# One layer (Mamba-2 mixer and top-2 LoRA feed-forward) on one core: in the first token block ScalarE makes the skip terms of chunks 2 and 3, and steps are put in another order

## What is computed

```
xn  = layernorm(x)
out = x + attn(xn) + ffn(xn)

attn: proj = xn @ in_proj_w.T            -> gate 4096, conv input 6144, dt 64
      xBC  = silu(conv4(conv input))     -> x (64 heads x 64), B, C (8 groups x 128)
      state_t = state_{t-1} * exp(dt A) + dt x_t B_t ;  y_t = state_t C_t
      y  = y + x * D                     (D: one number a head, the skip term)
      yn = rmsnorm over 512 (y) * norm_weight * silu(gate) ; attn = yn @ out_proj_w.T
ffn:  xn @ W_base.T + b + top-2 of 8 experts of rank 16 (scale 2)
```

## Time and profile before

| | us |
|---|---|
| median of three runs | 3119.39 (3118.51 to 3121.8) |
| the profiled execution, its own time | 3118.07 |
| its span in the trace | 3116.3 |
| TensorE busy | 3098.2 (99%) |
| VectorE busy | 2681.8 (86%) |
| ScalarE busy | 1787.1 (57%) |
| GpSimd busy | 813.7 (26%) |

### The profile page before, as it was taken

How to read it: one execution, slowest core, us unless ns; L and a number is a source line. 1 busy time by engine, 2 the same in 40 slices (tenths; PEclk the granted TensorE clock), 3 DMA queues, 4 the chain that set the end, 5 groups by cost and what they waited for, 6 DMA issues and landing times.

```text
span 3116.3 us, 55148 instructions
## 1 busy us (share of the span) xinstructions
PE 3098.2 (99%) x17392; PEld 2547.4 (82%) x17392; DVE 2681.8 (86%) x4675; ACT 1787.1 (57%) x4782; POOL 813.7 (26%) x833
## 2 busy tenths in 40 slices
PE   8999999999999999999999999999999999999999
PEld 7788888887888888888788888888878888888887
DVE  7998888987598999999759899999975899999984
ACT  5766666664256665566326666655633656666651
POOL 4444443434022222212203122222110211221210
PEclk9999999999999999999999999999999999999999
DMA  8777777776665555565566555555646655556554
GB/s 286 277 263 274 270 271 273 261 264 248 241 228 191 195 201 188 192 203 192 181 224 205 196 193 193 202 190 190 215 164 229 212 190 196 196 195 201 192 190 163
DMA packets 185670, 672.63 MB, mean 216 GB/s; under 512 B 21056, under 2 KB 22208, under 8 KB 185408
## 3 DMA queue, kind: packets, MB, share of 16 engines
q1 hardware_dynamic: 161280, 584.91, 53.8%
q10 hardware_dynamic: 24128, 84.42, 8.3%
HBM read 532.41 MB, written 136.84 MB: 215 GB/s over the span
## 4 chain that ended last, share of the span: by engine, by line
PE 90%; DVE 6%; ACT 2%; issue 1%; DMA 1%; SPq 0%; ACTq 0%; DVEq 0%
PE dense L1157 20%; PE dense L1159 19%; PE dense L1158 19%; PE pX L1157 7%; PE pX L1159 7%; PE pX L1158 7%; PE pY L1271 3%; DVE conv_us L1572 3%; PE pD L1271 1%; PE pCB L1244 1%; PE pS L1158 1%; PE pS L1157 1%; PE pS L1159 1%; PE pU L1157 1%; PE pU L1159 1%
## 5 line engine op out<-in xcount | busy, mean ns | idle before, releaser
L1157 PE MATMUL dense<-xn_hi,w_hl 128*128 128x512 f32 (+2 forms) x2192 | 868.3, 396 | 2.2 <-ACT conv_us L725 1.3
L1159 PE MATMUL dense<-xn_hi,w_hl 128*128 128x512 f32 (+2 forms) x2192 | 853.1, 389 | 0.0
L1158 PE MATMUL dense<-xn_lo,w_hl 128*128 128x512 f32 (+2 forms) x2192 | 851.9, 389 | 0.0
L1572 DVE SCALAR_TENSOR_TENSOR conv_us<-conv_in,const_g,conv_us 128x512 f32<-128x512 f32 x576 | 469.5, 821 | 30.2 <-ACT conv_us L725 18.4
L1157 PEld LDWEIGHTS dense<-xn_hi,w_hl 128*128 128x128 f32 (+1 forms) x2192 | 409.8, 187 | 92.5 <-ACT conv_us L725 4.8
L1159 PEld LDWEIGHTS dense<-xn_hi,w_hl 128*128 128x128 f32 (+1 forms) x2192 | 409.5, 187 | 88.1
L1158 PEld LDWEIGHTS dense<-xn_lo,w_hl 128*128 128x128 f32 (+1 forms) x2192 | 410.0, 187 | 85.8 <-issue 2.6
L1607 DVE STREAM_TRANSPOSE x_tm<-xBC 32x320 f32<-32x320 f32 x832 | 417.8, 502 | 12.8
L520 POOL TENSOR_TENSOR C_lo<-xBC,C_hi 128x128 fp32r<-128x128 f32 x120 | 66.0, 550 | 1207.6 <-ACT S_hi L768 1207.2
L1757 DVE STREAM_TRANSPOSE xBC<-yn 32x256 f32<-32x256 f32 x672 | 292.9, 436 | 77.9 <-ACT yn L845 67.6
L1157 PE MATMUL dense<-z_hi,w_hl 128*128 128x512 f32 x820 | 326.5, 398 | 1.9 <-DVE acc L1780 1.1
(11 more groups left out here) (239 smaller groups left out, 5673.5 us busy)
## 6 DMA issues: line engine op xcount, KB each, us to landing
w_hl<-w_split SPq DMA_DIRECT2D x732, 512.0 KB, 3.5
w_split<-w_hl SPq DMA_DIRECT2D x244, 512.0 KB, 3.8
cum_b<-cum_scratch ACTq DMA_DIRECT2D x128, 512.0 KB, 5.0
w_raw<-w_slots_dram SPq DMA_DIRECT2D x122, 512.0 KB, 5.5
acc<-x_tr_dram ACTq DMA_DIRECT2D x16, 512.0 KB, 6.5
out_tr_dram<-acc ACTq DMA_DIRECT2D x16, 512.0 KB, 4.7
xBC<-x_tok_dram SPq DMA_DIRECT2D x6, 512.0 KB, 5.3
conv_us<-x_tok_dram SPq DMA_DIRECT2D x6, 512.0 KB, 6.1
```

Of the source, the lines that this page charges most:

```text
L1157: nc.tensor.matmul(out, lhs[0], rhs[0], start=start, stop=False)
L1158: nc.tensor.matmul(out, lhs[0], rhs[1], start=False, stop=False)
L1159: return nc.tensor.matmul(out, lhs[1], rhs[0], start=False, stop=stop)
L1572: nc.vector.scalar_tensor_tensor(out=conv_u[r], in0=conv_in[r][:, t:t + TB], scalar=const_g[p][:, 4 * j + t:4 * j + t + 1], in1=conv_u[r], ...
```

## The change

It has four parts.

1. **Skip terms.** In block 0, for chunks 2 and 3 of groups 1 to 7, VectorE's one instruction of 128x512 (L1665) goes, and ScalarE makes the same xD by eight instructions of 128x64, one a head, the head's D as scale (`skip_one`). They stand behind `normalize` and ahead of the next `split`. That is 14 instructions less on VectorE and 112 more on ScalarE.
2. **Silu and evacuation.** In groups 1 to 6 VectorE runs the silu of unit j-1 ahead of the taps of unit j, and ScalarE the evacuation of unit j ahead of the tanh of unit j-1.
3. **Groups 1 and 7.** Group 1: ScalarE normalizes chunk 3 of group 0 before it evacuates gate unit 1, and makes its z_hi before the next split; VectorE makes its z_lo before the next low half, and its rounds of `x_rows` stand one each in the output units 1 to 3. Group 7: the rounds stand in the output units 0 to 2 instead of one ahead of them and two in them.
4. **End.** The last of the four stores is cut in two, one tile each.

The diff:

```diff
@@ -427,7 +427,7 @@
                 block_body(q, False, False)
             block_body(NQ - 1, False, True)
 
-            sp.wait_ge(out_stored, 16 + NQ * 64)
+            sp.wait_ge(out_stored, 16 + NQ * 64 + 16)
 
 
         @block.gpsimd
@@ -688,6 +688,9 @@
             nc.scalar.activation(A_neg[:], A_neg[:], ACT.Exp).then_inc(const_act, 1)
 
             def block_body(q, first_block, last_block):
+                def skip_by_act(g, c):
+                    return first_block and turned(g, c, first_block)
+
                 n_dt = 0
 
                 def dt_step(ins):
@@ -812,6 +815,8 @@
                     wx_high(g, c)
                     if c >= 1:
                         normalize(g, c - 1)
+                    if skip_by_act(g, c):
+                        skip_one(g, c)
                     next_cum(g, c, last)
 
                 def skip(g, c):
@@ -820,6 +825,14 @@
                     act.wait_ge(y_x, carry_n(q, g, c, False) - (1 if g == 1 and c == 0 else 2))
                     for h in range(HPG):
                         ins = nc.scalar.activation(xD_2[c % 2][:, h * P:(h + 1) * P], x_tm[:, c % 2, h * P:(h + 1) * P], ACT.Copy,
+                                                   scale=D_g[:, h:h + 1])
+                    ins.then_inc(xd_done, 1)
+
+                def skip_one(g, c):
+
+                    act.wait_ge(xt_done, xt_n(q, g, c, first_block))
+                    for h in range(HPG):
+                        ins = nc.scalar.activation(xD[:, h * P:(h + 1) * P], x_tm[:, c % 2, h * P:(h + 1) * P], ACT.Copy,
                                                    scale=D_g[:, h:h + 1])
                     ins.then_inc(xd_done, 1)
 
@@ -931,9 +944,9 @@
                             x_conv(j)
                             tanh_conv(g, j - 1)
                         elif not last:
+                            x_conv(j)
                             if j >= 1:
                                 tanh_conv(g, j - 1)
-                            x_conv(j)
 
                     def out_unit(m):
                         if not first:
@@ -943,8 +956,9 @@
                     if behind_first:
                         z_high(0, 2)
                         mean_square(0, 3)
-                        gate_unit(1)
+                        split(g, k_gate(first, 1))
                         normalize(0, 3)
+                        ev_gate(g, first, 1, p)
                     else:
                         if not first:
                             normalize(g - 1, 3)
@@ -952,8 +966,10 @@
                     chunk_1(g, p, 0, last)
                     if first:
                         load_residual(1)
+                    if behind_first:
+                        z_high(0, 3)
                     split(g, k_gate(first, 2))
-                    if not first:
+                    if not first and not behind_first:
                         z_high(g - 1, 3)
                     ev_gate(g, first, 2, p)
                     gate_unit(3)
@@ -1090,6 +1106,12 @@
                         paired_group(g, g % 2, second=g > 1)
                 (group if first_block else paired_group)(7, 1, last=True)
 
+                def store_tile(i):
+
+                    act.wait_ge(evac_dve, tail_n(q, i))
+                    act.dma_start(out_tr[bass.ds(q, 1), :, i:i + 1, :].rearrange("b p o t -> (b p) o t"),
+                                  acc[:, i:i + 1, :]).then_inc(out_stored, 16)
+
                 def store(m):
 
                     act.wait_ge(evac_dve, tail_n(q, 2 * m + 1))
@@ -1109,7 +1131,11 @@
                     ln_high(q + 1, 3)
                 store(1)
                 store(2)
-                store(3)
+                if last_block:
+                    store_tile(OT - 2)
+                    store_tile(OT - 1)
+                else:
+                    store(3)
 
             block_body(0, True, False)
             with act.Fori(1, NQ - 1) as q:
@@ -1661,6 +1690,8 @@
                     nc.vector.tensor_tensor(B_lo[:], pCB[:, 0:N], B_hi[:].bitcast(F32), ALU.subtract).then_inc(bl_done, 1)
 
                 def skip(g, c):
+                    if skip_by_act(g, c):
+                        return
                     dve.wait_ge(sq_done, chunk(q, g, c) + 1)
                     nc.vector.tensor_tensor(heads(xD[:]), heads(x_tok_of(g, c)), D_g[:].unsqueeze(2).broadcast_to([128, HPG, P]),
                                             ALU.mult).then_inc(xd_done, 1)
@@ -1907,10 +1938,12 @@
                             if m == 0:
                                 dve.wait_ge(acc_loaded, (q + 1) * 64)
                             out_adds(g, m, halves=(0,))
-                            if first_block and m < 2:
-                                x_rows(g, 2, p, 2 + m, 3 + m)
+                            row = m + (0 if behind_first else 1 if last else 2)
+                            if 1 <= row < 4:
+                                x_rows(g, 2, p, row, row + 1)
                             out_adds(g, m, halves=(1,))
-                            lo(g, K_OUT + m)
+                            if not (behind_first and m == 0):
+                                lo(g, K_OUT + m)
 
                     def x_low(j):
                         if last:
@@ -1919,9 +1952,9 @@
 
                     def x_conv(j):
                         if not last:
-                            conv_taps(g, j, p)
                             if j >= 1:
                                 silu(g, j - 1, 1 - p)
+                            conv_taps(g, j, p)
 
                     def x_unit(j):
                         x_low(j)
@@ -1953,6 +1986,8 @@
                         gate_tile(g, 0, first)
                         gate_tile(g, 1, first)
                     masked(g, 0)
+                    if behind_first:
+                        gated_lo(0, 3)
                     lo(g, k_gate(first, 2))
                     if not behind_first:
                         if not first:
@@ -1975,7 +2010,8 @@
                         consts_next(g, p)
                         router_top()
                     else:
-                        x_rows(g, 2, p, 1, 2)
+                        if not last and not behind_first:
+                            x_rows(g, 2, p, 1, 2)
                         lo(g, k_gate(first, 3))
                         chunk_2(g, 0)
                         gate_tile(g, 3, first)
@@ -1984,6 +2020,8 @@
                         if not last:
                             consts_next(g, p)
                         chunk_1(g, 1)
+                        if behind_first:
+                            lo(g, K_OUT)
                         out_unit(1)
                     masked(g, 1)
                     out_unit(2)
```

## The result

Before ran in 3119.55 us (median of 6 runs, 3118.04 to 3121.8), the changed kernel in **3132.01 us** (median of 6, 3130.3 to 3133.29). The ratio is 1.0038, 95% interval 1.0028 to 1.0048: slower, by 12.5 us. The profiled executions took 3118.07 and 3130.3 us, their spans are 3116.3 and 3128.5: +12.2 against a forecast of +11.4.

What follows compares the result with a forecast made beforehand. TensorE, busy 99% of the span, was taken to bound the kernel. 3118.07 + 14.7 - 1.8 - 0.8 - 0.7 = 3129.5 us, +11.4, so a median of about 3131, range 3115 to 3137.

Steps and rivals of the forecast that it cites:

- Chunk 3 and x5: Behind chunk 3, the evacuation of x3 ends at 306.2, so TensorE waits 2.0 us at x5, bounds 1.0 and 2.3.
- wx_hi: Chunk 2's skip makes VectorE's wx of chunk 3, and wx_hi, 1.0 us late (1.7 less 0.67 idle), bounds 0 and 1.3.
- Taps and end of the group: Taps of x3 start at 307.4, 3.5 us late; gate unit 0's evacuation ends at 325.1, gate unit 2 2.45 us late.
- +14.7 for six groups: Groups 1 to 6 each lose 2.45 us, every group starting chunk 2 in step again: +14.7 us, bounds +8.4 to +16.8.
- Group 1: At its start, waits for normalized y (0.7), z_lo (0.5 taken) and one add go: together -1.8 us (-1.3 to -2.3).
- z_lo's 1.0: Start of group 1: TensorE's 1.0 us loss for z_lo shrinks by between 0 and 1.0, taken as 0.5.
- Group 7: At its start, the wait for an add goes with one round of transposes less ahead: -0.8 us (0 to -0.8).
- The end: The last store, about 1.4 us, is halved by moving one tile: -0.7 us (0 to -0.7).
- Rival A: ScalarE keeps up, no new wait arises at x5, all listed waits go: 5.8 us gained, 3113.5; chance 0.13.
- Rival B: VectorE catches up before chunk 3, wx_hi is on time, only half the delay: +5.1 us, 3124.5; chance 0.12.
- C: New and removed waits cancel in each group, nothing measurable changes: 3119; chance 0.04.
- D: VectorE's lateness outlives the output units, further waits for adds appear, 0.5 us a group: +3, 3134; chance 0.11.

Runs made afterwards that it cites:

- experiment 2: The kernel before with only the skip terms moved to ScalarE, the change's other parts undone: 3139.26 us, ratio 1.0063.
- experiment 5: The changed kernel with ScalarE making the skip term of chunk 3 alone, that of chunk 2 staying on VectorE: 3122.0 us, ratio 1.0006.
- experiment 3: The changed kernel with ScalarE's eight skip instructions moved behind the evacuation of the first conv unit after the chunk: 3113.66 us, ratio 0.998.
- experiment 7: The changed kernel with one 128x512 instruction per skip term instead of eight, all heads scaled by the first head's D: 3115.42 us, ratio 0.9987.
- experiment 4: The changed kernel with the old order of silu and tanh, skip terms staying on ScalarE: 3138.59 us, ratio 1.0061.

## Why the prediction was right, step by step

- **Chunk 3 and x5.** Forecast: wx_hi 1.0 us late, x5 at 306.2 in the time frame of before. Measured: 300.75 for 299.74, and x5 at 308.97 - 2.67 = 306.3.
- **wx_hi: the size was right, its making only in part.** With the old order it is as worked out: in experiment 2 wx_hi stands 69.3 to 69.5 us into groups 2 to 6, before at 68.4. In the change z_hi was to stay where it was, and VectorE's 0.67 us of idle ahead of z_lo to be used up. But the load of a raw tile, which SyncE issues only behind VectorE's low half, was issued 1.65 us later in the group (285.60 - 234.03 against 281.28 - 231.36) and took 7.9 us to land instead of 5.9. The splits ahead of z_hi waited for it, and VectorE idled for 0.90 us:

```profile
293.56 1.16 ACT L656 ACTIVATE w_hl<-w_raw 128x512 fp32r<-128x512 f32 x2 [4.76 <-DMA w_raw<-w_slots_dram]
...
295.26 0.85 DVE L1777 TENSOR_TENSOR z_lo<-z_t,z_hi 128x512 fp32r<-128x512 f32 x1 [0.90 <-ACT z_hi L862]
```

  So the skip of chunk 2 cost 1.86 us (experiment 5), nearly its whole 1.91, and the new order, which I had given no part in it, brought wx_hi forward by 68.38 - 67.53 = 0.85. The difference is the 1.0 of the forecast; in the change that was luck.
- **Taps and end of the group.** Forecast: taps of x3 at 307.4, gate unit 2 at 325.1. Measured: 310.08 - 2.67 = 307.4 and 327.73 - 2.67 = 325.1. VectorE's wait ahead of the low half of x5 is 2.67 us, as foretold.
- **+14.7 for six groups was somewhat too much.** The forecast let every group start in step again. Group 2 does, which has no wait at its own gate unit 2. From group 3 on TensorE itself is late there (0.38 us as drawn), so less is left to wait for at x5: 1.82 us in group 2, then 1.39 to 1.55. The term was 2.45 and is 2.1; groups 2 to 6 came to 13.25 - 2.67 = 10.6 instead of 12.25.
- **Group 1 cost more.** Forecast 2.45 - 1.8 = 0.65 for the whole of it, measured 2.67. Its start gave 1.3 instead of 1.8 (TensorE is 0.10 us ahead of before at 138 us and 1.44 at 172): y normalized won its 0.7, of which 0.3 went at the unit behind it, but z_lo's 1.0 was nearly all kept, by another engine. Then x5 waited 2.9 us (2.66 as drawn), not 2.0, because wx_hi was 2.0 us late and not 1.0: it starts at 209.84 (209.24 before) where TensorE is 1.44 ahead; why group 1 differs was not traced. Behind this wait the granted clock fell (below), 1.5 us that no step of mine had. The old wait at gate unit 1 gave 0.5 back and small ones took 0.2: -1.4 + 0.2 + 2.9 + 1.5 - 0.5 = 2.7. I had written that GpSimd's work could be in the way; it is, as TensorE's and GpSimd's timelines show:

```profile
150.92 1.15 PE L1297 MATMUL pY<-dtx,E 128*64 128x64 f32 x32
152.79 0.47 PE L1183 MATMUL dense<-z_hi,w_hl 128*128 128x512 f32 x1 [0.72 <-POOL w_hl L463]
...
150.84 3.51 POOL L463 TENSOR_TENSOR w_hl<-w_raw,w_hl 128x512 fp32r<-128x512 f32 x2
```

  GpSimd's half of the output unit's weights starts behind its wx_lo. Two such halves take 3.51 us, so the first ends at about 152.6, and the unit starts at 152.79.
- **Group 7** gave 13.25 - 12.84 = 0.4 of the 0.8, its own gate unit 2 being late first. **The end** gave 0.6 of 0.7.
- In sum 2.67 + 10.6 - 0.4 - 0.6 = 12.2 for 0.65 + 12.25 - 0.8 - 0.7 = 11.4. The total is nearer than its terms, by luck: a term too high by 1.7 and one too low by 2.0 met. The path (the eight in ScalarE's line, the wait at x5, the late end of the group) is what the rows show.
- **Rival A** (3113.5) was the value of the change with its skip elsewhere: experiment 3 gave 3113.66. The Trainium skill ("Perfetto Trace Analysis", Optimizing Scalar/DVE Operations) says that offloading from a saturated VectorE may pay; by that rule alone the change is a gain, and the runs show a loss of 17.5 us in one place of the queue and none in another. Rival B fell with wx_hi, which did not catch up, and C with the waits; D's further waits for adds did not come.

## What to carry to other kernels

Before work is given to an engine with a low busy share, find on its timeline the instruction that a third engine waits for next, and compare the slack there with what is put ahead of it. Take the slack with the rest of the change in place: here it was 1.8 us and not 0.4, against 1.9 us for the skip of chunk 3 and 1.9 more by the lateness that the skip of chunk 2 makes. If it doesn't fit, move it behind that instruction: here the same eight instructions cost 17.5 us ahead of the evacuation and nothing behind it. The eight instructions hold ScalarE for 1.91 us where the single one of experiment 7 held it for 0.61, and two delays, of which the slack hides nearly one but not both, cost more together than their sum.

## What the runs showed of the hardware that was not expected

The granted clock of TensorE fell for a short while behind the longest of the new waits. Busy time by stretches of the changed kernel, group 1: the wait, what follows, and after it (us; PE, PEld, DVE, ACT, POOL busy with instructions; granted clock; share and rate of the DMA engines).

```profile
212.50:215.38 2.88, 0.22 (x4) 0.00 (x1) 1.32 (x1) 2.88 (x10) 1.26 (x1) 0.97 0.02 9
215.38:218.80 3.42, 3.42 (x8) 2.71 (x9) 2.90 (x4) 2.93 (x7) 1.28 (x1) 0.53 0.89 313
218.80:222.00 3.20, 3.20 (x15) 2.63 (x14) 2.96 (x6) 0.92 (x2) 0.00 (x0) 1.00 0.97 330
```

The clock is 0.53 in the middle one, close to half, 1.2 GHz of 2.4, and back to 1.00 behind it. TensorE's timeline there:

```profile
215.38 0.79 PE L1183 MATMUL dense<-xn_hi,w_hl 128*128 128x512 f32 x1 [2.66 <-ACT conv_us L728]
215.97 0.63 PE L1184 MATMUL dense<-xn_lo,w_hl 128*128 128x512 f32 x1
216.40 0.63 PE L1185 MATMUL dense<-xn_hi,w_hl 128*128 128x512 f32 x1
...
222.47 0.39 PE L1183 MATMUL pU<-wx_hi,B_hi 128*128 128x512 f32 x1
```

and before:

```profile
213.74 0.47 PE L1157 MATMUL dense<-xn_hi,w_hl 128*128 128x512 f32 x1
...
219.31 0.39 PE L1157 MATMUL pU<-wx_hi,B_hi 128*128 128x512 f32 x1
```

Matmuls start 0.43 us apart instead of 0.23. From the start of x5 to what follows it are 222.47 - 215.38 = 7.09 us, before 219.31 - 213.74 = 5.57: the fall costs 1.5 us, half as much again as the wait itself. The waits of 1.39 to 1.82 us in the other groups had nothing of the kind behind them. In experiment 2 it came three times; this is what follows the wait in the second:

```profile
497.90:501.30 3.40, 3.40 (x9) 2.66 (x9) 3.33 (x4) 1.15 (x3) 1.32 (x1) 0.50 1.02 307
```

x5 takes 7.2 us there each time, 1.6 more than before. Not all of it stays in the time: groups 4 and 6, with a fall, are 3.6 and 3.7 us longer than before, groups 2, 3 and 5, without one, 2.7 to 2.9, of which a part is a wait at gate unit 1 that the other two do not have. That leaves about 0.85 us a fall, three times 0.85 = 2.6 us of 3139.26. It is an estimate from one execution.

In the same execution the waits before the three falls are 2.28, 2.30 and 2.30 us as drawn, and waits of 2.49, 2.29 and 2.29 us had no fall behind them; in experiment 5 one followed a wait of 2.02 us, in group 1. So the length of the wait alone does not settle whether the clock falls; what does was not tried. For a forecast this much follows: of 14 waits of 2 us or more in the profiled executions of the change and of experiments 2, 4 and 5, 8 had a fall behind them, which cost 1.5 to 1.6 us there and less by the end of the group; those up to 1.8 us had none.
